# Where the four value-product steps of a head pair stand in TensorE's order

## The reference

```
h = layernorm(x) * (1 + ca) + sa
q, k, v = h @ Wq.T, h @ Wk.T, h @ Wv.T          # split into 16 heads of 64
q, k = l2norm(q) * q_scale, l2norm(k) * k_scale
p = softmax(q @ k.T / 8)                        # 512 x 512 for each batch and head
x = x + ga * ((p @ v), heads joined, @ Wo.T + bo)
```

## Time and profile before

| | |
|---|---|
| median of three runs | 1470.58 us |
| span of the profiled execution, first to last instruction | 1467.0 us |
| TensorE matmuls busy | 1343.3 us, 92% |
| VectorE busy | 1103.4 us, 75% |
| ScalarE busy | 1058.0 us, 72% |
| GpSimd busy | 645.9 us, 44% |
| value steps, line 556 | 1024 matmuls, 275.7 us, 617 ns each |
| TensorE clock, mean granted | 0.967 |

### The profile page before, as it was taken

One profiled execution on the slowest core, in us unless ns is written; L12 is line 12 of the kernel. 1 busy time (PEld: TensorE's weight loads), 2 busy tenths in 40 slices (PEclk: granted clock), 3 DMA queues, 4 the chain that ended last, 5 costly groups with the idle time before them and its releaser, 6 DMA issues. The chain is left out here.

```text
span 1467.0 us, 27427 instructions
## 1 busy us (share of the span) xinstructions
PE 1343.3 (92%) x7114; PEld 913.1 (62%) x7114; DVE 1103.4 (75%) x2179; ACT 1058.0 (72%) x2650; POOL 645.9 (44%) x1279
## 2 busy tenths in 40 slices
PE   4699999999999999999999999999998377899997
PEld 4566666666665666666566666666654255677775
DVE  4478768776886787688768876876874798588887
ACT  3577868876887687688768877876875366677776
POOL 2245435543534454344336433443433666344443
PEclk8799999999999999999999999999999599899999
DMA  5344334543334344333435433354334000534331
GB/s 126 87 106 111 87 87 93 120 95 85 89 88 99 80 111 106 88 87 87 98 82 113 100 90 87 87 118 100 86 87 115 1 0 0 119 88 98 89 91 39
DMA packets 90054, 129.05 MB, mean 88 GB/s; under 512 B 12816, under 2 KB 55320, under 8 KB 89880
## 3 DMA queue, kind: packets, MB, share of 16 engines
q1 hardware_dynamic: 88696, 126.67, 38.3%
q10 hardware_dynamic: 1184, 0.40, 0.1%
HBM read 24.16 MB, written 2.23 MB: 18 GB/s over the span
## 5 line engine op out<-in xcount | busy, mean ns | idle before, releaser
L814 DVE TENSOR_REDUCE neg_max<-bank 128x1 f32<-128x512 f32 x512 | 350.2, 684 | 219.1 <-PE bank L525 212.5
L687 ACT ACTIVATE probs<-bank,neg_max 128x512 f32<-128x512 f32 x512 | 354.1, 692 | 144.1 <-DVE neg_max L814 139.5
L534 PEld LDWEIGHTS bank<-ident,probs 128*128 128x128 f32 x2048 | 236.1, 141 | 243.2 <-issue 150.0
L534 PE MATMUL bank<-ident,probs 128*128 128x128 f32 x2048 | 322.7, 280 | 1.9 <-ACT probsT L695 1.9
L556 PE MATMUL bank<-probsT,v_tok 128*64 128x512 f32 x1024 | 275.7, 617 | 0.9 <-DVE probsT L821 0.9
L524 PE MATMUL bank<-operands 128*128 128x512 f32 x512 | 236.8, 462 | 30.9 <-DMA operands<-operands 14.6
L50 POOL TENSOR_TENSOR rn_t<-rn 128x16 f32<-128x16 f32 x192 | 43.0, 224 | 367.5 <-DVE rn L41 357.5
L525 PE MATMUL bank<-operands 128*128 128x512 f32 x512 | 203.9, 398 | 0.0
L821 DVE COPY probsT<-bank 128x512 f32<-128x512 f32 x256 | 173.7, 678 | 0.6 <-PE bank L534 0.6
L661 ACT ACTIVATE qk_tok<-bank 128x256 f32<-128x256 f32 x256 | 99.1, 387 | 97.2 <-PE bank L494 96.8
L695 ACT ACTIVATE probsT<-bank 128x512 f32<-128x512 f32 x256 | 153.6, 600 | 11.3
(11 more groups left out here) (214 smaller groups left out, 2609.0 us busy)
## 6 DMA issues: line engine op xcount, KB each, us to landing
operands<-operands SPq DMA_DIRECT2D x256, 384.0 KB, 6.4
probsT<-gate_scratch SPq DMA_DIRECT2D x64, 256.0 KB, 5.0
out<-x_all SPq DMA_DIRECT2D x8, 256.0 KB, 2.4
probsT<-in_L_ffn_fc_w SPq DMA_DIRECT2D x1, 1024.0 KB, 8.9
raw<-in_L_attn_Wq SPq DMA_DIRECT2D x1, 512.0 KB, 4.6
raw<-in_L_attn_Wk SPq DMA_DIRECT2D x1, 512.0 KB, 7.5
raw<-in_L_attn_Wv SPq DMA_DIRECT2D x1, 512.0 KB, 8.8
raw_o<-in_L_attn_Wo SPq DMA_DIRECT2D x1, 512.0 KB, 8.9
```

The costliest lines, as they stand in the source:

```text
L534: last = nc.tensor.transpose(T_BANK[i % 2][:, j * P:(j + 1) * P], probs[:, i % 4, j * P:(j + 1) * P], ident[:])
L687: nc.scalar.activation(probs[:, i % 4], S_BANK[i % 3][:], ACT.Exp, bias=neg_max[:, i:i + 1], accum_out=row_sum[:, hp % 2, i:i + 1]).then_i ...
L814: nc.vector.reduce_max(neg_max[:, i:i + 1], S_BANK[i % 3][:], AX.X, negate=True).then_inc(max_done, 1)
```

## The change

In TensorE's slots 4 to 7 one value step each was issued between the scores and the transposes. Now slot 4 issues all four, between its scores and its transposes, and slots 5, 6 and 7 issue none. No other engine's program is changed.

```
--- before.py
+++ after.py
@@ -601,8 +601,9 @@
                         for i in range(S_TILES):
                             if main:
                                 scores(u, hp, i)
-                            if tail and i >= S_TILES - NT:
-                                weigh_values(u - 1, hp - 1, i - (S_TILES - NT))
+                            if tail and i == S_TILES - NT:
+                                for j in range(NT):
+                                    weigh_values(u - 1, hp - 1, j)
                             if tail and i < P_LAG:
                                 transpose_probs(u - 1, S_TILES - P_LAG + i)
                             if main and i >= P_LAG:
```

## The result

The changed kernel takes 1538.87 us (median of 4 runs, 1534.66 to 1541.41) against 1470.53 for the kernel before in the same comparison: a ratio of 1.0462, 95% interval 1.0443 to 1.0481. It is slower; the forecast was 1518 in a range from 1468 to 1546.

The account below looks back on a forecast made before the run. TensorE was taken as the bound, busy 780 of 800 us, with VectorE and ScalarE at three quarters. Terms 23.4, 17.4, 13.7, -6.3 and 0 for the jumps made +48 on 1470.6: 1518 us, range 1468 to 1546.

Parts of the forecast that it names:

- pair 1 of batches 1 to 7 (projection): Seven pairs with the output projection in slots 5 and 6 keep TensorE's saving: 7 x -0.90 = -6.3 us.
- plain pairs and the two ends: 21 pairs without extra VectorE work cost +0.65 us each, 13.7; the first and last pair change nothing.
- pair 2 of batches 1 to 7: VectorE's statistics put its cast behind GpSimd's multiplication: +1.67 us a pair.
- pair 3 of batches 1 to 7, pair 4 of batches 0 to 6: VectorE's layer norm rows make its cast late: +1.67 us a pair, less 0.43 for four transposes vanishing in the wait.
- pair 5 of batches 0 to 6: VectorE's split of the new input puts its cast behind GpSimd's multiplication: +1.67 us a pair.
- five loop jumps: Pair boundaries at the hardware loop's jumps: 0 in the sum, between -0.9 and +1.67 us each.
- TensorE's saving and the landing: Of 0.90 us saved a pair, 0.86 becomes a wait for the next pair's stacked operands to arrive.
- GpSimd: Row maximum 5 comes 2.21 us later, GpSimd's normalisation ends at 12.01 after slot 4, and TensorE's transposes wait 0.38.
- The cast: VectorE's cast starts 0.13 us ahead of GpSimd's multiplication; a pair costs +0.4 to +0.83 then, +1.67 if second.
- rival A: VectorE's cast comes second everywhere, so the 21 plain pairs cost 1.67 us too: +69, 1540; chance 0.15.
- Rival C: Waiting for the stacks to arrive replaces what TensorE saves, and nothing else is late: 1453 us; chance 0.11.

Follow-up runs that it names:

- experiment 5: Kernel before, with the query third of the stacks shipped when the queries are there, eight transfers for four: 1452.45 us, ratio 0.9882.
- experiment 6: Changed kernel with two bursts of two value steps in slots 4 and 6, and the query third of the stacks shipped early: 1456.99 us, ratio 0.9913.
- experiment 1: Changed kernel with the norms' two VectorE instructions ahead of row maximum 5 instead of behind it: 1482.92 us, ratio 1.0086.
- experiment 2: Kernel before, without the burst, with the norms' two VectorE instructions moved ahead of row maximum 5: 1470.49 us, ratio 0.9999.
- Experiment 3: Changed kernel with the high half of the values computed once more from the bank instead of cast: 1511.69 us, ratio 1.0279.
- Experiments 7: Kernel before with the hardware loop over batches 1 to 6 written out: 1441.33 us, ratio 0.9802.
- experiment 8: Changed kernel with the norms ahead of row maximum 5 and the loop over batches 1 to 6 written out: 1444.14 us, ratio 0.9816.

## Why the prediction was right, and where it was short

It was right in sign and mechanism, and short by 21 us. From the start of slot 4 to the next one, summed over the pairs, the changed kernel loses 68.2 us of attention against 48 forecast:

| term | forecast | measured |
|---|---|---|
| pair 1 of batches 1 to 7 (projection) | -6.3 | -6.1 |
| plain pairs and the two ends | +13.7 | +14.0 |
| pair 2 of batches 1 to 7 | +11.7 | +10.2 |
| pair 3 of batches 1 to 7 | +8.7 | +16.0 |
| pair 4 of batches 0 to 6 | +8.7 | +9.9 |
| pair 5 of batches 0 to 6 | +11.7 | +4.2 |
| five loop jumps | 0 | +20.0 |

The jumps alone make up the shortfall, and that is in part luck: pair 3 came out 7.3 above its term and pair 5 7.5 below. The 14.0 of the plain pairs is luck too: pair 0 of batches 1 to 6, counted among them, holds 8.1 of it, where 0.65 each makes 3.9.

*TensorE's saving and the landing.* Slot 5 at 4.64 for 4.65, next scores at 8.65 for 8.65, with a wait for the transfer ahead of them. The saving does turn into this wait, and experiments 5 and 6 show that shipping earlier takes it away.

*GpSimd.* Row maximum 5 at 5.38 (5.39 forecast), the multiplication at 10.08 (10.10). It ends at 12.20, 0.19 later than forecast, since it takes 2.12 and not 1.91: it loses 0.2 of the cast's 0.43. A plain pair costs 0.48, between the bounds 0.4 and 0.83 and below the 0.65 taken; experiments 1 and 2 show that the norms' lateness, which makes GpSimd's result and the casts late, cost 56 us.

*The cast.* At 10.01 (9.97 forecast), first by 0.07: the tie fell as forecast, narrowly, and rival A with it. Experiment 3 shows the blocked casts at 27 us. But the list of blocked pairs was off. Pair 5 isn't blocked: there the multiplication starts 0.6 behind the cast, at 10.62 in pair 29. In that pair the Newton steps that start amid VectorE's split of the new input and amid the cast take 0.36, 0.55 and 0.28 where they take 0.21 to 0.22 in pair 30. And pair 0 of batches 1 to 6 is blocked, at 1.23 to 1.43 a pair; it has copies of the scales in slot 5, which the list left out. In batch 7, which is written out, the same copies come without the register work that the loop's addresses need, row maximum 6 starts at 6.72 and not at 7.25, and the cast, at 10.02, is free.

*Pair 3.* The forecast let the four layer-norm transposes vanish in the wait, worth 0.43. They are among the 14 new waits of line 585, 0.42 each. And it overlooked a consumer: the query transposes of pair 4 also wait for the router's logits, which VectorE takes from their bank behind the blocked cast and the next pair's first row maximum. In batches 1 to 6 TensorE stands idle for 1.59 there; these are the "issue" waits of line 502 (batch 4, VectorE's logits and TensorE):

```profile
695.52 0.17 DVE L865 TENSOR_TENSOR z_all<-bank,projb_row 128x32 f32 x1
...
695.80 0.63 PE L502 MATMUL bank<-ident,qk_tok 128*128 128x128 f32 x4 [1.59 <-issue]
```

1.59 and 0.42 are the 2.0 that such a pair loses. Twice TensorE came back from this idle stretch at the lower clock (pair 3 of batches 4 and 6: 3.6 instead of 2.0). This term was mis-sized by 7 us.

*The jumps* are the step that failed. The sum has "the five jumps 0, between -0.9 and +1.67 each": each measured 2.9 to 4.7, outside the bounds. I bounded them by what pairs cost, and not by what a jump itself does: the trace before shows a gap of 14.2 us in five jumps, with the stacks' transfer under it, and I asked only when TensorE would be there, not what its instructions would meet. Experiments 7 and 8 show the term.

Rival C, the other side, needed GpSimd's result only 0.4 earlier. Experiment 1 brings it more than 2 us forward (it ends at 9.29 in pair 30), and even then C doesn't come true: 1483, because of the jumps, and without them (experiments 8 and 7) 1444 against 1441. There TensorE waits more for landings (42 times, 23.8 us, against 7 times, 12.6 us) and 18 times, 8.5 us, for ScalarE's exponentials.

The upper end of the range was meant as rival A with the jumps lost too; by its own terms that is about 1548, not 1546. Nothing hangs on it.

## What to carry to other kernels

Closing up matmuls on the engine that bounds a kernel moves everything that stood between them; before doing it, write down who has its input from the delayed slots and by how much it was early (here 1.87 us, for a delay of 2.21), and move those consumers' work first. A shorter burst kept most of what could be had: two bursts of two gained 2.0% over single steps (1403 against 1432) once norms, transfers and loop were out of the way, the burst of four lost 0.4%. (The single steps kept the norms where they were.) And a jump of a hardware loop is a place of its own in a sum: look at what is being transferred when the engines reach it.

## What the runs showed of the hardware

- GpSimd's multiplication loses time behind VectorE's cast as the cast does behind it: started 0.07 after a cast of 0.43, it took 2.12 where it takes 1.90 undisturbed. The Trainium skill (SBUF — State Buffer, "SBUF: two separate sides") has the second to come blocked for the other's whole instruction; the cast's 1.62 behind the multiplication agrees, while GpSimd loses 0.22, less than the 0.36 that were left of the cast. The rows of the changed kernel fit a full block that ends 0.14 to 0.15 ahead of the recorded end of VectorE's instruction: the 20 multiplications that start amid a cast, and the slowed Newton steps of pair 5, all lose what was left of it but that much, and a blocked cast ends 0.28 behind the multiplication, 0.15 less than its free 0.43.
- Sixteen value matmuls in one run take 3.65 us, so a step behind another adds 0.86 each time, as the two in the drained tail did.
- Five jumps of the loop cost 29 us in the kernel before, though the gaps that the waits show add up to 14.2. By the starts of the first scores, writing the loop out took 14.9 us from the pairs that end with a jump and 5.8 from those behind one; the rest came from other pairs and from behind attention.
